# A four-layer graph kernel: weights and block limits made during the scatter, ranks added in a tree, 16-bit type coefficients and clears, outputs by chunk

## What is computed

```python
h = relu(layernorm(x)); x = x + relational(h)   # two passes
#   W[r] = sum_b a[r, b] V[b]     (8 bases)
#   out[dst] = sum over edges of h[src] @ W[type] + h @ loop + bias
h = relu(layernorm(x)); x = x + segment_sum(h[src], dst)
h = relu(layernorm(x)); x = x + flow(h)         # two edge MLPs, one node MLP
h = relu(layernorm(x)); x = x + attention(h)    # 4 heads of 8
#   softmax over the edges of each dst, then @ Wo
```

## Time and profile before

| What | us |
|---|---|
| median of three runs | 4336.23 |
| lowest, highest run | 4322.93, 4382.05 |
| the profiled execution | 4388.69 |
| its span, first to last instruction | 4386.9 |
| PE busy | 2724.1 (62%) |
| DVE busy | 2517.4 (57%) |
| POOL busy | 2404.2 (55%) |
| ACT busy | 560.0 (13%) |
| mean granted clock of TensorE | 0.744 of full speed |

### The profile page before, as it was taken

How to read it: one execution, slowest core, us unless ns; L and a number is a source line. 1 busy time by engine, 2 the same in 40 slices (tenths; PEclk the granted TensorE clock), 3 DMA queues, 4 the chain that set the end, 5 groups by cost and what they waited for, 6 DMA issues and landing times. The chain is left out here.

```text
span 4386.9 us, 58293 instructions
## 1 busy us (share of the span) xinstructions
PE 2724.1 (62%) x19425; PEld 1832.1 (42%) x19425; DVE 2517.4 (57%) x7425; ACT 560.0 (13%) x1352; POOL 2404.2 (55%) x2308
## 2 busy tenths in 40 slices
PE   0220002888995888755765899999997455555551
PEld 0100002666763666544543555555554222222221
DVE  9000004888844788755655566666664466666667
ACT  0000000000010000000000222222221222222220
POOL 3777775667417766277775444444442444444440
PEclk9555555777756777777777899999997666766675
DMA  5110002111121111111111000000000000000010
GB/s 83 35 38 26 7 7 61 21 22 21 13 87 17 21 21 22 13 18 16 20 18 14 9 10 9 10 9 10 9 9 11 18 17 18 17 17 18 18 15 4
DMA packets 126307, 91.00 MB, mean 21 GB/s; under 512 B 60182, under 2 KB 111958, under 8 KB 125398
## 3 DMA queue, kind: packets, MB, share of 16 engines
q0 software_dynamic: 72192, 41.76, 7.0%
q1 hardware_dynamic: 53846, 45.58, 4.5%
HBM read 59.77 MB, written 27.41 MB: 20 GB/s over the span
## 5 line engine op out<-in xcount | busy, mean ns | idle before, releaser
L683 POOL DMA_INDIRECT rel_rows<-message_table,message_indices x640 | 676.8, 1057 | 426.6 <-issue 178.0
L1239 POOL DMA_INDIRECT flow_x<-node_table,flow_index x440 | 421.2, 957 | 511.1 <-DVE flow_index L1254 391.4
L1604 POOL DMA_INDIRECT att_kv_rows<-kv_table,att_index x440 | 420.6, 956 | 444.1 <-DVE att_index L1615 315.4
L746 DVE TENSOR_SCALAR rel_source_onehot<-rel_sources,node_numbers 128x384 bf16<-128x384 f16 x2000 | 504.9, 314 | 179.4 <-remote 135.4
L1376 PE MATMUL flow_acc_bwd<-flow_onehot_j,flow_by_q 128*128 128x512 bf16 x2640 | 574.1, 337 | 0.0
L822 PE MATMUL p_rel_picked<-rel_source_onehot,rel_h_parts 128*96 128x384 bf16 x2000 | 471.6, 408 | 78.7 <-issue 76.7
L379 POOL DMA_INDIRECT sorted_edges<-stage,sorted_row x416 | 426.8, 1026 | 160.3 <-issue 126.9
L989 POOL DMA_INDIRECT sum_rows<-node_table,src_indices x320 | 405.8, 1268 | 125.7 <-issue 94.5
L1640 DVE TENSOR_REDUCE att_tile_max<-p_att_scores 128x4 f32<-128x512 f32 x440 | 292.5, 687 | 253.6 <-PE p_att_scores L1754 169.6
L822 PEld LDWEIGHTS p_rel_picked<-rel_source_onehot,rel_h_parts 128*96 128x96 bf16 x2000 | 306.7, 157 | 240.9 <-issue 104.3
L1023 DVE TENSOR_SCALAR sum_source_onehot<-sum_sources,node_numbers 128x384 bf16<-128x384 f16 x1000 | 245.8, 310 | 167.0 <-remote 129.5
(11 more groups left out here) (288 smaller groups left out, 4792.0 us busy)
## 6 DMA issues: line engine op xcount, KB each, us to landing
message_table<-message_rows SPq DMA_DIRECT2D x50, 320.0 KB, 2.1
rel_rows<-message_table,message_indices POOLq DMA_INDIRECT x640
rel_sources<-source_rows SPq DMA_DIRECT2D x80, 96.0 KB
flow_x<-node_table,flow_index POOLq DMA_INDIRECT x440
att_kv_rows<-kv_table,att_index POOLq DMA_INDIRECT x440
sorted_edges<-stage,sorted_row POOLq DMA_INDIRECT x416
sum_rows<-node_table,src_indices POOLq DMA_INDIRECT x320
sorted_edges<-records SPq DMA_DIRECT2D x1, 4400.0 KB, 12.9
```

Of the source, the lines that this page charges most:

```text
L683: pool.indirect_dma_start(out=rows[b][:, t, :], out_offset=None, in_=d["messages"], in_offset=bass.IndirectOffsetOnAxis(ap=s["idx_msg"][:, ...
L746: last = dve.tensor_scalar(which[g % 2][:, c, :], srcs[b][:], s["node"][:, c:c + 1], None, ALU.is_equal)
L1239: pool.indirect_dma_start(out=X[b][:, t, 0:F], out_offset=None, in_=d["nodes"], in_offset=bass.IndirectOffsetOnAxis(ap=ibuf[b][:, t:t + 1] ...
L1604: pool.indirect_dma_start(out=KV[b][:, t, :], out_offset=None, in_=d["kv"], in_offset=bass.IndirectOffsetOnAxis(ap=ibuf[b][:, t:t + 1], ax ...
```

## The change

The weights of both relational layers are made by DVE in the scatter's block, the first before the table stage, the second after it; both sets of inputs are loaded in the sort. The block limits (`begin`, `end`, `keep`, `anyt`) are made there as well, and kept. In the sort the tile map's first half stands ahead of the 25 rank instructions, and the strided reduction is six additions. In the relational passes the type one-hots are 16-bit and the coefficients three 16-bit parts (nine products for three). `clear_acc` uses 16-bit operands. In the join, the products with Wo follow each turned chunk. Some scratch tiles of the sort lie in the tiles that are now kept.

```diff
+            "begin": sb(ctx, "block_begins", [P, T]),
+            "end": sb(ctx, "block_ends", [P, T]),
+            "keep": sb(ctx, "block_goes_on", [P, T]),
+            "anyt": sb(ctx, "any_tile_rows", [P, NB]),
...
-                sort_edges(nc, a, s, d, sb, ps, sem)
-                relational_layers(nc, a, s, d, sb, ps, sem)
+                s["w_term"] = sb(first, "w_rel_term", [F, R, F])
+                second = relation_weights(a, s, sb, sem, first, 2)
+                sort_edges(nc, a, s, d, sb, ps, sem, second)
+                relational_layers(nc, a, s, d, sb, ps, sem, second)
...
                     load_weights(sp)
+                    second[1](sp)
...
                     pool.memset(s["rec"][:, :, DSTL:DSTL + 1], -1.0).then_inc(recs, 1)
-                    make_weights(pool)
...
                     v.done(dve.tensor_scalar(off[:], off[:], -1.0, None, ALU.add))
+                    dve.wait_ge(cols, 2)
+                    v.done(dve.tensor_copy(uptoc[:], pcol[0:NB, 0:1]))
+                    dve.wait_ge(consts, 11)
+                    dve.tensor_scalar(past, tno, uptoc[:, 0:1], None, ALU.is_ge).then_inc(tmap, 1)
                     for b in range(NB):
                         last = dve.scalar_tensor_tensor(out=rank[:, b, :], in0=rank[:, b, :],
                                                         scalar=off[:, b:b + 1], in1=mask[:, b, :],
                                                         op0=ALU.add, op1=ALU.mult)
                     v.done(last)
-                    v.done(dve.tensor_reduce(blk[:], rank[:].rearrange("p b c -> p c b"), AX_X, ALU.add))
+                    for lo, n in ((12, 12), (6, 6), (3, 3), (2, 1), (1, 1)):
+                        v.done(dve.tensor_tensor(rank[:, 0:n, :], rank[:, 0:n, :], rank[:, lo:lo + n, :], ALU.add))
+                    v.done(dve.tensor_tensor(blk[:], rank[:, 0, :], rank[:, NB - 1, :], ALU.add))
...
-                    dve.wait_ge(cols, 2)
-                    v.done(dve.tensor_copy(uptoc[:], pcol[0:NB, 0:1]))
-                    dve.wait_ge(consts, 11)
-                    dve.tensor_scalar(past, tno, uptoc[:, 0:1], None, ALU.is_ge).then_inc(tmap, 1)
                     dve.wait_ge(tmap, 2)
...
+            tiles = block_limits(s, sb, ps, sem, st2)
...
+                    make_weights(dve)
                     front["dve"](dve)
+                    second[2](dve)
+                    tiles["dve"](dve)

                 @block.tensor
                 def _(pe):
                     front["pe"](pe)
+                    tiles["pe"](pe)
...
+def block_limits(s, sb, ps, sem, st):
+
+
+    dblk = sb(st, "tile_blocks", [1, T])
+    edge = sb(st, "block_edges", [1, 2 * T])
+    po = [ps(st, f"p_limits{i}", [P, BANK]) for i in range(2)]
+    vs, ready, rep = (sem(st, f"limits_{n}") for n in ("steps", "ready", "replicated"))
+
+    def dve_part(dve):
+        v = Steps(dve, vs)
+        v.done(dve.tensor_copy(dblk[:], s["dcol"][:, 1, :]))
+        v.done(dve.memset(edge[:], NEG))
+        v.done(dve.tensor_tensor(edge[:, 1:T], dblk[:, 1:T], dblk[:, 0:T - 1], ALU.not_equal))
+        v.done(dve.tensor_scalar(edge[:, 1:T], edge[:, 1:T], NEG, None, ALU.mult))
+        dve.tensor_copy(edge[:, T:2 * T - 1], edge[:, 1:T]).then_inc(ready, 1)
+        dve.wait_ge(rep, 1)
+        v.done(dve.tensor_copy(s["begin"][:], po[0][:, 0:T]))
+        dve.tensor_copy(s["end"][:], po[1][:, 0:T])
+        dve.tensor_scalar(s["keep"][:], s["begin"][:], 0.0, None, ALU.is_equal)
+        dve.tensor_copy(s["anyt"][:], po[0][:, T:T + NB])
+
+    def pe_part(pe):
+        pe.wait_ge(ready, 1)
+        pe.matmul(po[0][:, 0:T], s["ones"][0:1, :], edge[:, 0:T], start=True, stop=True)
+        pe.matmul(po[0][:, T:T + NB], s["ones"][0:1, :], s["any_tile"][:], start=False, stop=True,
+                  skip_group_check=True)
+        pe.matmul(po[1][:, 0:T], s["ones"][0:1, :], edge[:, T:2 * T], start=True, stop=True).then_inc(rep, 1)
+
+    return {"dve": dve_part, "pe": pe_part}
...
-    Wt = sb(st, f"w_rel_term{layer}", [F, R, F])
+    Wt = s["w_term"]
...
-            kinds = [sb(st1, f"{name}_type_onehot{b}", [R, RW]) for b in range(2)]
+            kinds = [sb(st1, f"{name}_type_onehot{b}", [R, RW], BF16) for b in range(2)]
...
-            ab = sb(st1, f"{name}_type_coef", [R, NBASIS])
+            ab = sb(st1, f"{name}_type_coef", [R, 3, NBASIS])
...
                     v.done(split_parts(dve, v, V[:]))
+                    v.done(split_parts(dve, v, ab[:]))
                     dve.sem_inc(parts_ready, 1)
...
-                        if g == 0 and "dve" in parts:
-                            parts["dve"](dve)
...
                         for t in range(RPT):
-                            last = pe.matmul(pc[:, t * NBASIS:(t + 1) * NBASIS], kinds[g % 2][:, t * P:(t + 1) * P],
-                                             ab[:], start=True, stop=True)
+                            for j in range(3):
+                                last = pe.matmul(pc[:, t * NBASIS:(t + 1) * NBASIS], kinds[g % 2][:, t * P:(t + 1) * P],
+                                                 top(ab[:])[:, j, :], start=(j == 0), stop=(j == 2))
                         last.then_inc(coef_done, 1)
...
-        pe.matmul(bank, s["ones"][0:1, :], zeros[0:1, :], start=True, stop=True, skip_group_check=True)
-
-
-def relational_layers(nc, a, s, d, sb, ps, sem):
-    def layer(k, after, load=None, **more):
+        pe.matmul(bank, s["identb"][0:1, :], zeros[0:1, :].bitcast(BF16)[:, 0:BANK], start=True, stop=True,
+                  skip_group_check=True)
...
-                    if load:
-                        load(sp)
...
-                    v.done(dve.tensor_copy(dblk[:, 0:T], s["dcol"][:, 1, :]))
-                    v.done(dve.memset(edge[:], NEG))
-                    v.done(dve.tensor_tensor(edge[:, 1:T], dblk[:, 1:T], dblk[:, 0:T - 1], ALU.not_equal))
-                    v.done(dve.tensor_scalar(edge[:, 1:T], edge[:, 1:T], NEG, None, ALU.mult))
-                    dve.tensor_copy(edge[:, T:2 * T - 1], edge[:, 1:T]).then_inc(e_ready, 1)
-                    dve.wait_ge(rep, 1)
-                    v.done(dve.tensor_copy(begin[:], po[:, 0:T]))
-                    v.done(dve.tensor_copy(end[:], po[:, BANK:BANK + T]))
-
-                    v.done(dve.tensor_scalar(keep[:], begin[:], 0.0, None, ALU.is_equal))
-                    v.done(dve.tensor_copy(anyt[:], pa[:, 0:NB]))
...
-                    pe.wait_ge(e_ready, 1)
-                    pe.matmul(pa[:, 0:NB], s["ones"][0:1, :], s["any_tile"][:], start=True, stop=True)
-                    pe.matmul(po[:, 0:T], s["ones"][0:1, :], edge[:, 0:T], start=True, stop=True)
-                    pe.matmul(po[:, BANK:BANK + T], s["ones"][0:1, :], edge[:, T:2 * T], start=True, stop=True)\
-                        .then_inc(rep, 1)
+                    def outputs(c):
+                        pe.wait_ge(taken, c + 1)
+                        for b in range(4 * c, min(4 * c + 4, NB)):
+                            last = pe.matmul(po[:, b * F:(b + 1) * F], aT[:, b * P:(b + 1) * P], Wo[:],
+                                             start=True, stop=True)
+                        return last
+
                     pe.wait_ge(att_ready, 1)
                     for c in range(TURNS):
                         if c >= 2:
...
                             last = pe.transpose(pt[c % 2][0:F, (b % 4) * P:(b % 4 + 1) * P], att[:, b, :],
                                                 s["ident"][:])
                         last.then_inc(turned, 1)
-                    pe.wait_ge(taken, TURNS)
-                    for b in range(NB):
-                        last = pe.matmul(po[:, b * F:(b + 1) * F], aT[:, b * P:(b + 1) * P], Wo[:],
-                                         start=True, stop=True)
-                    last.then_inc(o_done, 1)
+                        if c >= 1:
+                            outputs(c - 1)
+                    outputs(TURNS - 1).then_inc(o_done, 1)
```

35 lines of the change are left out of this document (15 added, 20 removed).

## The result

The changed kernel takes 4372.5 us (median of 20 runs, 4345.2 to 4426.8). The kernel before takes 4346.6 in the 20 runs beside it. The ratio is 1.0049, with a 95% interval of 1.0027 to 1.0071: 21 us slower, where the prediction had 65 us faster and a range up to 4322. The ratio leaves out, of each kernel, the executions more than 1.5% above its fastest, so it can differ from the quotient of two medians, which are of all executions. The profiled execution took 4375.5, with a span of 4373.7 and a granted clock of 0.743.

A forecast was written before the change was run, and what follows sets the result against it. No one engine was taken to bound the kernel; its stages stand behind each other. Terms 23.8 + 2 + 25 + 4 + 8.6 + 2.1 - 0.7 = 65 us, so 4336 - 65 = 4271 us, range 4218 to 4322.

The forecast's parts named there:

- Sort: Sort block on DVE: small steps 3.4, rank instructions 12.7, tree 6.0 and a wait 1.7, together 23.8 us less.
- Scatter: POOL's scatter DMAs beside DVE's 30 moved weight instructions: no cost; bound 24 us more if each holds POOL throughout.
- The first pass's start: First relational pass: PE's wait behind DVE's 15 weight instructions goes, 2 us less; bounds 0 and 12.
- Clears: Flow layer's clear on PE with 16-bit operands: 4 us less; bounds 0 and 5.4.
- Join: Block-limit steps from 4284.85 to 4293.48 leave the join: 8.6 us less.
- Outputs: Join's turns and products by chunk: 12.6 us in place of 14.7, 2.1 less.
- The coefficients: Relational passes: nine 16-bit products save PE 0.44 us a group, 70% counted, 25 us less; bounds 61 less, 30 more.
- Rival 3: Relational and sum passes: faster PE frees POOL's buffers sooner, more stalls at 41 us each; 4353 with two; chance 0.08.
- Rival 4: Moved weights slow POOL's scatter by 24 us in place of the 20 given back in the sort; chance under 0.05.
- Rival 1: Relational passes: the coefficients bring nothing, as DVE's next wait or the clock takes the gain; 4296; chance 0.22.
- Rival 2: Shifted timing avoids one stall of some 41 us and the coefficients give all 35; 4220; chance 0.20.

The follow-up runs named there:

- e9: Kernel before with only DVE's source one-hots split into 9 segments in place of 5: 4315.6 us, 0.9926 of the kernel before.
- e10: Changed kernel with DVE's source one-hots in 9 segments in place of 5 and float32 type coefficients: 4271.4 us, 0.9804 of the kernel before.
- e2: Kernel before with only the type coefficients changed to nine 16-bit products, on the first chip: 3767.5 us, 1.0116 of the kernel before.
- e1: Changed kernel with only the type coefficients put back to float32, on the first chip: 3693.8 us, 0.9899 of the kernel before.
- e8: Changed kernel with float32 coefficients and the join's output products all behind the last turn: 4321.8 us, 0.9937 of the kernel before.
- e7: Changed kernel with DVE's 25 source one-hots in 9 segments in place of 5: 4266.8 us, 0.9804 of the kernel before.
- e6: Changed kernel with two more float32 products on PE in each group, lengthening PE's step: 4368.8 us, 1.0030 of the kernel before.
- e5: The changed kernel run again, unaltered, on a later chip: 4376.2 us, 0.9987 of the kernel before.
- e11: Changed kernel with 9 one-hot segments and 3 buffers of gathered rows in place of 6: 4221.8 us, 0.9706 of the kernel before.
- e15: Changed kernel with 3 buffers of gathered rows in place of 6, five segments kept: 4318.8 us, 0.9850 of the kernel before.
- e12: Changed kernel with one small memset more on DVE behind each 16-bit type one-hot: 4380.6 us, 1.0046 of the kernel before.
- e14: Changed kernel with two more float32 products on PE and one more DVE memset per group: 4358.1 us, 0.9970 of the kernel before.
- e13: Changed kernel with the three 16-bit coefficient parts stacked, three products in place of nine: 4358.7 us, 0.9986 of the kernel before.

## Why the prediction was wrong

**Sort, 23.8:** right in sum (24.5 in e9 against e10) and in each term: 3.4 for the small steps; 12.7 for the rank instructions, whose cause was POOL's weights; 6.0 for the tree at 11.5 us. The wait went.

**Scatter, 0, bound 24 worse:** the value was a little off and the bound held. 13 DMAs beside the weights took 1.39 in place of 0.96, 5.6 us together; 1.6 of it stands at the scatter's end. The row I argued from, DMAs beside the norm at 957 to 962, was one lucky stretch: in the changed kernel one such DMA takes 1.73 (96.71). From one DMA to the next beside the weights are 1.69 us, which is two of DVE's instructions (0.845 apart), so a DMA gets on between two of them, and is not held for all thirty. The Trainium skill, "SBUF — State Buffer", section "Who interferes with whom", has an instruction with two SBUF inputs contend with a GpSimd instruction that reads SBUF, but says too that such additions (`tensor_tensor`) were not seen to stall a DMA; I had gone by the rows beside the norm. The measurement decides: 1.39 for 0.96, a delay, and a small one.

**The first pass's start, 2, bounds 0 and 12:** from the first to the last group of the first pass, ACT's copies take 463 us in e9 and 456 in e10, so some 7 with the weights out of the way. 5 too little, inside the bounds.

**Clears, 4, bounds 0 and 5.4:** the first hidden activation of the flow layer comes 10.0 us earlier, where its first gather comes 1.8 earlier: 8.2 (9.0 between the same two in e9 and e10, 4.2 between e2 and e1 on the first chip). On the later chips that is over the upper bound: what stands behind the clear profits as well. **Join, 8.6:** right.

**Outputs, 2.1 less:** wrong in sign, 2.9 more. A turn was taken at a product's 0.165 against its own row's 0.23, and came at 0.24. A product's 0.165 was a mean over two levels of the clock, 0.11 us at 1.00 and 0.20 at 0.50; beside turns, at 0.50 throughout, it came at 0.23.

**The coefficients, 25 less, bounds 61 less to 30 more:** the step that failed. The price of the nine products was right (0.31 for 0.32), and it is the inference from it that was wrong: "nothing hides it", and 70% of 0.44 us a group. In its place the runs showed a cost: 43 us on the first chip (e2), some 47 on the later ones (e8 against the first comparison), where the two passes lost 72 in the trace; and nothing with nine segments (e7, e10). I had read the earlier trace rows, DVE waits for PE, as: PE is late, so a faster PE helps. But PE was late by idle time with no wait in the trace, 152 us of the two passes, and that time grew to 228 when PE's step fell. On the first chip it was another thing: POOL had no room (eight gathers at 1048 ns with 0.30 between are 10.8 us of a group of 11.0 in e1), its gathers got longer beside DVE's one-hots, and PE came to wait for rows. I had put POOL beside PE and DVE in the first view and not asked what its gather takes beside DVE's one-hots.

**The range, 4218 to 4322,** was too narrow by its own terms: it takes the coefficients as 25 worse at most, that is as worth nothing, where their own bound was a loss of 30; and the bounds that it names, with one stall each way, add up to 4205 to 4341. The measured 4372.5 is outside these too.

**The rivals.** Rival 3 named the place and the sign, at 0.08, and its argument against, that POOL's pace beside PE's hardly changes, was a statement about lengths where what counts is how two rhythms meet. Its price, whole stalls of 41 us, was not how it came: the stall at the second pass's start was there before (67.8 and 63.6 us), and most of the loss is in many groups of 17 to 23. Rival 4's 20 us given back in the sort are 16.1 by the terms of the sort (3.4 and 12.7). Rival 1, the coefficients bring nothing, holds with nine segments. Rival 2 did not come. The clock did not cause it: it was granted at 0.743 against 0.744 over the span, and a pick took 402 ns against 408.

**What is shown and what is open.** Shown by runs: the 16-bit coefficients are what makes the change slow (e2 on the first chip, beside the kernel before; less firmly e8 on a later one, which lies clear below the first comparison and e6, but not below e5); with nine segments the long gathers go (e7, e9), and the coefficients' harm with them (e7 and e10); a pass's slow start shortens with the number of gathers that POOL can issue at once (e11, e15). Shown by the traces: on the first chip the time goes where PE waits for gathered rows, on the later ones where PE stands without a wait. Argued, not shown: that the long gathers are the link on the later chips too. They and the idle time of PE mostly rise and fall together there, but PE hardly ever waits for a row. Nine segments were not run on the first chip. Open: which part of the coefficients' edit does it. PE's length alone (e6) and DVE's alone (e12) do not bring the time back; both together (e14) and the number of products (e13) could not be told from the changed kernel. Open too is what makes an instruction wait in steps of 0.70 us.

## What to carry to other kernels

Where two engines hold each other up, how their rhythms meet can set the pace, and a saving on a third engine can spoil it: before taking a saving as time, look at the spread of one instruction's length (0.94, 1.31, 2.91 here), not at its median, and at what the late engine waits for; idle time without a wait is not time that a shorter instruction gives back. Try to break up long runs of the instructions that hold the other engine; here one constant took the changed kernel from 1.0049 to 0.9804 of the kernel before. Give a DMA-issuing engine only as many buffers as the steady state needs: the lead is issued in one burst at the start, and on the later chips here the other engines all but stood while it lasted.
